# Two-layer macaron block on one core: PSUM banks from a common pool, and the string of steps placed anew

## The chip, the cores and the metric

One core of one Trainium2 chip. The metric is the time of one execution of the program on the device, in microseconds; three runs of the kernel before gave 803.5 to 805.67 us, with a median of 804.64 us.

## The reference, cut to what matters

The input is x of shape (2, 1024, 128), two sequences of 1024 rows. Six residual steps follow each other (`ln` is the layer norm):

```python
x = x + 0.5 * int8_linear(ln(x))              # layer 0: quantised rows, 128x128 weights
x = x + causal_attention(ln(x), H=16, d=8)    # with rotary positions
x = x + 0.5 * int8_linear(ln(x))
x = x + 0.5 * down(silu(gate(ln(x))) * up(ln(x)))   # layer 1: 128 -> 384 -> 128
x = x + causal_attention(ln(x), H=16, d=64)
x = x + 0.5 * down(silu(gate(ln(x))) * up(ln(x)))
```

The two attentions are most of the work: 2 x 16 heads of 1024 x 1024 scores each, of which the lower triangle counts.

## The kernel before, in words

Rows are put in 8 tiles of 128. A start written out by hand (up to about 37 us) takes sequence 0 through the first linear layer and the projections of layer 0; an end written out by hand does the last products of pair 15 and the last FFN of sequence 1. Between them stands `PLAN`, a list of 985 steps. All engines walk this same list in order, and each does its own part of a step: TensorE fills a slot of PSUM, ScalarE ("A") and VectorE ("V") read it, GpSimd and the DMA queues (SP) do what belongs to it. The order comes from the string `ORDER`: each letter takes the next step of its own stream (`streams`).

Layer 0's attention works on 8 groups of 4 heads, layer 1's on 16 pairs of heads (2 sequences x 8). Scores come in 9 chunks of 1024 columns (in a group, twice 9: two heads each):

- `gkq` (a), `gmax` (m), `gturn` (t), `gexp` (e), `gweigh` (w), `gheads` (g): keys and queries turned; scores filled (L1207) and their maxima taken by VectorE (L1054); the maxima turned and moved by DMA into the queries; scores filled once more and exponentiated by ScalarE (L811); their product with the values (L1156), which gathers in bank 7; the heads turned back (L1389).
- `pq`, `pk`, `pv` (Q, K, V), `max` (M), `turn` (T), `exp` (E), `weigh` (W), `sum` (S), `wo` (O): the same for a pair: projections (L1398, L1403), maxima (L1081), exponentials (L840), product with the values (L1177) in banks 6 and 7, sums of exponentials that GpSimd adds up (L672) and TensorE sums over rows (L1238), the output product (L1435). The reciprocals of the sums go out to DRAM and come back spread over the partitions (`reciprocals`, L456, L462), and GpSimd multiplies (L518).
- `h`: the steps of norms (`ln`), linear layers (`xq`, `imm`), rotary positions (`rope`), FFN (`xt`, `up`, `down`) and so on, which lead from one attention to the next: sequence 1's first layers, then 0's middle, 1's middle, and 0's last FFN.

PSUM has 8 banks of 512 fp32 columns. Before, banks 0 to 5 are a ring of three slots of two banks (`RING`), which all steps with readers take in turn, one-bank ones too; bank 6 is a side slot for `gturn`, `gheads`, `xq` and `scale` as long as layer 1's products don't need it (`ON_SIDE`, up to step 457, the first `weigh`). TensorE waits before each fill until the readers of the slot's user before are done:

```python
before = user_before(n)          # three users back in the ring, one back on the side
if before is not None:
    for e in PLAN[before][3]:
        pe.wait_ge(slot_seen[e], READS[e][before])
```

A reader takes the slot's 1024 columns in one instruction, `up` and `gkq` excepted, whose halves go to different places. `KEEP` names steps ahead of which some matmuls (L1246) are put in whose result isn't used.

## Time and profile before

| | |
|---|---|
| time, median of three runs | 804.64 us |
| profiled execution, span | 798.2 us |
| TensorE matmuls busy | 725.3 us, 91% |
| VectorE busy | 532.1 us, 67% |
| ScalarE busy | 450.9 us, 56% |
| GpSimd busy | 466.8 us, 58% |
| instructions | 21288 |

The span goes from the first to the last instruction of one profiled execution; the runs' times hold some 6 us more around it. The engines' shares are means over stages of different kinds, so the rows below take stretches apart. A matmul's busy time overlaps that of the next one, as they are pipelined.

### The profile page before, as it was taken

Reading aid. Unit: us, or ns where it says so; the run is one execution under the profiler, and the core shown is the slowest. Engines: PE = TensorE matmul, PEld = TensorE weight load, DVE = VectorE, ACT = ScalarE, POOL = GpSimd, SP = SyncE. Lnnn points to the kernel's source line nnn. Section 1 sums busy time; section 2 is a strip of 40 time slices with the busy share of each in tenths; the row PEclk is TensorE's granted clock in tenths of the full one; section 3 lists DMA queues with packets and bytes.
Section 4 is the critical chain, followed back from the end, with each engine's and each line's share of the span. In section 5 each row is a group of like instructions: output and inputs, shape, how many; then the busy total and the mean of one; then the engine's idle time right before and its main releaser. Section 6 shows DMA issues by size and latency. Waiting matters only on the chain.

```text
span 798.2 us, 21288 instructions
## 1 busy us (share of the span) xinstructions
PE 725.3 (91%) x9393; PEld 429.3 (54%) x9406; DVE 532.1 (67%) x704; ACT 450.9 (56%) x495; POOL 466.8 (58%) x367
## 2 busy tenths in 40 slices
PE   3667888888888899998999999999999999999997
PEld 1533454445335444554565565555776655676764
DVE  7699967889778765777675575556536556753037
ACT  2424769986575689555636655665444665546312
POOL 6815567600850300499968777877655986667840
PEclk9855989999899999999999999999999999999999
DMA  8000000000000000000001111001101101111110
GB/s 271 2 1 2 3 2 3 2 3 2 2 2 2 2 3 2 2 2 5 27 4 26 29 30 29 10 22 28 30 2 28 29 3 29 29 29 30 28 29 26
DMA packets 13223, 16.18 MB, mean 20 GB/s; under 512 B 3052, under 2 KB 10572, under 8 KB 13132
## 3 DMA queue, kind: packets, MB, share of 16 engines
q1 hardware_dynamic: 12556, 14.50, 6.3%
q8 instruction: 74, 1.21, 0.6%
q10 hardware_dynamic: 576, 0.33, 0.2%
q14 instruction: 17, 0.14, 0.1%
HBM read 13.26 MB, written 1.17 MB: 18 GB/s over the span
## 4 chain that ended last, share of the span: by engine, by line
PE 70%; DVE 17%; POOL 5%; ACT 5%; issue 3%; DMA 0%; ACTq 0%; POOLq 0%; DVEq 0%
PE ps L1228 19%; PE ps L1177 16%; DVE big L1054 9%; PE ps L1156 6%; PE ps L1398 5%; PE ps L1207 5%; PE ps L1435 3%; ACT Pr L811 3%; PE ps L1403 2%; PE ps L1352 2%; PE ps L1238 2%; POOL acts L672 1%; DVE moments L1004 1%; PE ps L1346 1%; PE ps L1318 1%
## 5 line engine op out<-in xcount | busy, mean ns | idle before, releaser
L1081 DVE TENSOR_REDUCE mxb<-ps 128x8 f32<-128x1024 f32 x144 | 173.3, 1222 | 90.4 <-PE ps L1228 61.3
L672 POOL TENSOR_TENSOR V0s<-V0s,Pr 128x1024 f32<-128x1024 f32 x77 | 182.1, 2365 | 62.7 <-ACT Pr L840 31.0
L1054 DVE TENSOR_REDUCE big<-ps 128x8 f32<-128x1024 f32 x144 | 168.9, 1218 | 27.9 <-PE ps L1207 16.6
L811 ACT ACTIVATE Pr<-ps,exp_scale 128x1024 f32<-128x1024 f32 x144 | 154.8, 1114 | 44.4 <-PE ps L1207 31.5
L840 ACT ACTIVATE Pr<-ps,exp_scale 128x1024 f32<-128x1024 f32 x112 | 119.5, 1114 | 90.3 <-PE ps L1228 72.9
L1228 PE MATMUL ps<-big 64*128 64x128 f16 (+2 forms) x2560 | 168.9, 259 | 0.7 <-DVE mxb L1081 0.4
L1207 PE MATMUL ps<-big 32*128 32x128 f16 (+2 forms) x1280 | 102.4, 279 | 35.7 <-DVE big L1054 22.2
L1228 PEld LDWEIGHTS ps<-big 64*128 64x128 f16 x2560 | 92.8, 94 | 71.6 <-issue 17.0
L1177 PE MATMUL ps<-Pr,V1s 128*64 128x128 f32 (+2 forms) x960 | 111.3, 371 | 0.0
L1207 PEld LDWEIGHTS ps<-big 32*128 32x128 f16 x1280 | 40.4, 95 | 108.5 <-DVE big L1054 53.1
L587 POOL TENSOR_TENSOR stats<-moments 128x8 f32<-128x8 f32 x9 | 1.9, 210 | 163.7 <-DVE moments L1004 163.7
L684 ACT ACTIVATE big<-ps 128x1024 f16<-128x1024 f32 (+3 forms) x63 | 51.9, 826 | 71.0 <-PE ps L1398 28.2
L672 POOL TENSOR_TENSOR acts<-acts,Pr 128x1024 f32<-128x1024 f32 x35 | 82.5, 2357 | 13.2 <-ACT wkqv_s L823 4.0
L1156 PE MATMUL ps<-Pr,V0s 128*18 128x128 f32 (+2 forms) x1280 | 82.1, 382 | 0.2 <-ACT Pr L690 0.2
L1177 PEld LDWEIGHTS ps<-Pr,V1s 128*64 128x64 f32 x960 | 56.0, 136 | 37.1 <-issue 24.7
L1077 DVE TENSOR_TENSOR big<-ps,big 128x1024 f16<-128x1024 f32 x32 | 39.1, 1223 | 34.4 <-ACT big L684 33.6
L1228 PE MATMUL ps<-big,shr_s 64*128 64x256 f16 (+2 forms) x384 | 55.8, 287 | 0.0
L518 POOL TENSOR_TENSOR big<-Pr,rec_b 128x1024 f32<-128x1024 f32 x15 | 35.5, 2363 | 17.6 <-DMA rec_b<-scratch_dram 7.5
L1398 PE MATMUL ps<-XT,wqkv 128*128 128x512 f16 x192 | 45.3, 380 | 0.0
L1156 PEld LDWEIGHTS ps<-Pr,V0s 128*18 128x18 f32 x1280 | 30.4, 100 | 20.2 <-issue 13.2
L840 ACT ACTIVATE V0s<-ps,exp_scale 128x1024 f32<-128x1024 f32 x22 | 24.5, 1114 | 18.2 <-PE ps L1218 17.0
L1398 PEld LDWEIGHTS ps<-XT,wqkv 128*128 128x128 f16 x192 | 17.6, 98 | 22.0 <-ACT Pr L840 1.7
(242 smaller groups left out, 921.7 us busy)
## 6 DMA issues: line engine op xcount, KB each, us to landing
rec_b<-scratch_dram SPq DMA_DIRECT2D x30, 256.0 KB, 3.9
X<-in_x_dram SPq DMA_DIRECT2D x2, 256.0 KB, 3.8
big<-in_pick_rows_dram SPq DMA_DIRECT2D x2, 256.0 KB, 3.0
X<-in_x_dram SPq DMA_DIRECT2D x1, 512.0 KB, 5.4
rec_b<-in_w_q_dram SPq DMA_DIRECT2D x1, 512.0 KB, 5.8
XT<-in_w_k_dram SPq DMA_DIRECT2D x1, 512.0 KB, 6.6
XT<-in_w_v_dram SPq DMA_DIRECT2D x1, 512.0 KB, 7.3
wo_s<-in_w_o_dram SPq DMA_DIRECT2D x1, 512.0 KB, 8.1
```

Source lines behind the costliest of these rows:

```text
L672: g.tensor_tensor(dst, dst, src, ALU.add).then_inc(summed, 1)
L684: a.activation(dst, src, ACT.Copy).then_inc(slot_act, 1)
L811: a.activation(group_buf[e_no % GROUP_BUFS], by_head(slot), ACT.Exp, scale=exp_scale[0][:, 0:1]).then_inc(slot_act, 1)
L840: a.activation(dst, by_head(slot), ACT.Exp, scale=exp_scale[1][:, 0:1]).then_inc(slot_act, 1)
L1054: v.tensor_reduce(maxima_of(mall[:, r, 2 * u:2 * u + 2], i), block_view(by_head(slot), i), AX.X, ALU.max, negate=True).then_inc(slot_dve, 1)
L1077: v.tensor_tensor(low, slot, high, ALU.subtract).then_inc(slot_dve, 1)
L1081: v.tensor_reduce(maxima_of(mxb[:, r], arg), block_view(by_head(slot), arg), AX.X, ALU.max, negate=True).then_inc(slot_dve, 1)
L1156: ins = te.matmul(ps[HR * j:HR * j + 2 * VW, 7, a0 - 512 * half:a1 - 512 * half], values(g // GB, t, GH * (g % GB) + j, half), src, start= ...
L1177: ins = te.matmul(ps[h * D1:(h + 1) * D1, 6 + bank, a0 - 512 * bank:a1 - 512 * bank], V1[p % SETS][:, t, h * D1:(h + 1) * D1], src, start= ...
L1207: ins = te.matmul(slot[:, 512 * h + off:512 * h + off + a1 - a0], still[rows, tile(t)], moving[rows, a0:a1], start=q == 0, stop=cut is Non ...
L1228: ins = te.matmul(slot[:, 512 * h + off:512 * h + off + a1 - a0], still[rows], moving[rows], start=q == 0 and k == 0, stop=not goes_on and ...
L1398: ins = te.matmul(slot[:, cols], w16[:, ww], x16[:, xx, cols], start=part == 0, stop=part == 2)
```

## The change

All banks but 7 are in a pool, a list of banks, dealt in turn while the list of steps is walked, before anything runs; a step takes one bank (`ONE_BANK`) or two from its front, and puts them at its end. From the first `weigh` on bank 6 is left out. Since two banks taken one after the other needn't be neighbours, a slot is now a list of banks; readers of a whole slot read it in one instruction if the banks are neighbours in rising order, else in two (`whole`, `copy_whole`). TensorE waits for the last users of each bank (`wait_for_banks`). `v` is read in two halves always. The string `ORDER` and the list `KEEP` are new; the steps in it are the same ones, 985 in all.

```diff
-RING = 3
-SIDE = "gturn", "gheads", "xq", "scale"
+ACC0, ACC1 = 7, (6, 7)
+ONE_BANK = "gturn", "gheads", "xq", "scale", "turn", "sum", "wo"
 ORDER = (
-    "ammmmmmmmammmmmmmmmmmmmtmmmeehmmmaememhehehwmemhwemwmememmeewmhmehwemhwemewtehmmwememewhmeaeewmhmmhm"
-    "hewmemwememgehhhmhhemtwehmeewemewmemhehmhhehwmewmhmwmeamegemeweemwmhwemewmemmeewemmteewmememwmemwmew"
-    "memgeaemewmemwemwememmeewemewemmwemtemwemwmememwmeegmmhmmhhemhwemwmemhehwemewaeehtemwmemwemmmeheehwe"
-    "hmwemwhemhewmemememwewemewmheagemhhhhwhhewmememmhtemwehemwmememmwemhememmhewegemwemwmemwememeweeewtQ"
-    "eKweeweewMeweegMweeVMeweMewMeewMeweeVMweeMwMwgTKhQhEhMEhMWMEWMEEMWMMEWEMhhKQWVMEWTMhMEWWEMWMEMWEMWME"
-    "WhMEEhhVShhEMQKWTWEEMWMMWWMEMWMEEhEEWhhEWhhVhhEMWMQhhKShMWMEMWTEMWWMEMWWEMEWWWMEEEMWMSWThKQVWMEEEMWW"
-    "MEMWMEEEEEEMWWMMMWSQKVTWWWMEMWMEEMWWMESMEMWMMVKQTWWEEEMWMEMWEEMWWEMWWMEMWMEEEEMWWSTQKVWWMEEEEMWMWMMW"
-    "WMEEEEEMWWMEEMSKQVTWWWWMEEMWWMMWEEEKEMWWMEEMWWMMQSWWTMEEMWMMEWWEMVVOMEEEMWSMEEEMWOKOTQOMEMWWWWMMEhWW"
-    "WMEEMWMMEWMEESQKVThWWMEMWMEEMWWMEMWWMEEEEhVWSMEMWWTQhhWKEWEMEhEMWWMMMWWSMEEEEhhWWWMEEMWMhKQVTWWMEEMW"
-    "MWMEMWMEEEKWWMEMWMEQThVEMSEMMWWWMEEMWWWMEEMWWMEEEMWWWTSEEEEWWWWEEEEEESWWOOOOEEWWWWWWW"
+    "ammmmmmmmammmmmmmmmmamtmmehememmmmwhhheemmemmememwmemwememewemhtmhemwheewwehmheweewmeamemememwhemwme"
+    "mwemmhmwmhmehmeewmemememwtmehwmehhhmhmewmemwehmgeemwemewemmwhmhehmgwemeaewheememewmemhwtmehwmememaem"
+    "wmemwememememwememegwhemewmewmemwemwmtememememwemwemegemwhmmhheeweawmememmewhememewhthemwemwmememwme"
+    "hmmewmemhemhewmwemheehweawmemmeememwememehtmmhwemwhhehhhwhewegmehheweeemwemewmhewemewmememwemwemhwem"
+    "eQtKKQewegeMeweMeMeweMewMeewMeweMeweMwMeVegewTQwMgVEMEhEMWWMEMWEMhEEEMWMEWhhMKKVMWhTMWMSWMhEWhEMQWMW"
+    "EVEWMEMWMEMWTMEMWhMEEWMMQEWWhhEEWEMWMMKEWEMWMWMESEhTVMWMWMMEhWEMQKWEEMEWMWTVWEMEWMEMWSWMhEEWEMMWhhWE"
+    "KhEWVMhWhWEhEEWQMhMEWhWTSEMWEMQEKWMhSWEMEMEMWWMMEWMEEMWMWTEEhWEWWMWMEEEQEEWMKMWSWMWMMEWTWEMVEWWMEMWE"
+    "MVEQMWKEWMWEEMWMEWSMTVEEMWMMWQEMWWMEEVEMWEMWKEWEMSMWMWMEWTEMWQEMWWMEEEKEWSMMWMOWMVTEWMOMWEEOMEOMWMEM"
+    "WWMMQKWSEEMWWTEMWEhEEEMWEMMWEQWWWMMVWMEEKWMWhESEWEWTMWMEMWMEEMWhEWVWEhKEWEEMWMEMWMEQhWSWTMEMWMEMWMVM"
+    "WEMWEhWMVEMEEKhWEQSTEWMMWEWMEMWMMWWMEWMEhWEEWMhWEESEWTEEWhWWWEWEEEEWWOEWEESOWWEWOOWWW"
 )
 KEEP = {
-    ('gmax', 1, (7, 1)): 2,
-    ('gmax', 5, (1, 0)): 1,
...
+    ('gexp', 0, (0, 0)): 3,
+    ('gmax', 3, (8, 0)): 2,
+    ('gexp', 2, (6, 1)): 3,
+    ('gexp', 3, (8, 0)): 2,
+    ('gexp', 4, (8, 1)): 2,
+    ('gmax', 6, (4, 1)): 2,
+    ('gmax', 7, (0, 0)): 2,
+    ('gmax', 7, (4, 0)): 2,
 }
-def user_before(n):
-
-    users, back = (SIDE_USERS, 1) if ON_SIDE[n] else (USERS, RING)
-    k = users.index(n) - back
-    return users[k] if k >= 0 else None
+def deal_banks():
+
+    free = [bank for bank in range(8) if bank != ACC0]
+    user, banks_of, users_before = {}, {}, {}
+    for n, (kind, key, arg, readers) in enumerate(PLAN):
+        if (kind, key, arg) == ("weigh", 0, 0):
+            free = [bank for bank in free if bank not in ACC1]
+            users_before[n] = [user[bank] for bank in ACC1 if bank != ACC0]
+        if not readers:
+            continue
+        count = 1 if kind in ONE_BANK else 2
+        taken, free = free[:count], free[count:] + free[:count]
+        banks_of[n] = sorted(taken)
+        users_before[n] = [user.get(bank, -1 - bank) for bank in taken]
+        user.update((bank, n) for bank in taken)
+    return banks_of, users_before
...
+        def whole(n):
+
+            taken = BANKS_OF[n]
+            if taken[1] == taken[0] + 1:
+                return [(slice(0, 2), ps[:, taken[0]:taken[0] + 2, :])]
+            return [(slice(k, k + 1), ps[:, taken[k]:taken[k] + 1, :]) for k in range(2)]
...
+            def copy_whole(n, dst, func=ACT.Copy, scale=1.0):
+
+                act.wait_ge(slot_filled, SLOT_NO[n] + 1)
+                for part, src in whole(n):
+                    ins = a.activation(dst[:, part], src, func, scale=scale)
+                ins.then_inc(slot_act, 1)
...
                 if kind == "gexp":
...
-                    act.wait_ge(slot_filled, SLOT_NO[n] + 1)
-                    a.activation(group_buf[e_no % GROUP_BUFS], by_head(slot), ACT.Exp,
-                                 scale=exp_scale[0][:, 0:1]).then_inc(slot_act, 1)
+                    copy_whole(n, group_buf[e_no % GROUP_BUFS], ACT.Exp, exp_scale[0][:, 0:1])
...
                 if kind == "gmax":
...
-                    v.tensor_reduce(maxima_of(mall[:, r, 2 * u:2 * u + 2], i), block_view(by_head(slot), i), AX.X,
-                                    ALU.max, negate=True).then_inc(slot_dve, 1)
+                    for part, src in whole(n):
+                        ins = v.tensor_reduce(maxima_of(mall[:, r, 2 * u:2 * u + 2][:, part], i), block_view(src, i), AX.X,
+                                              ALU.max, negate=True)
+                    ins.then_inc(slot_dve, 1)
...
+            def wait_for_banks(n):
+
+                for e in "AV":
+                    seen = [READS[e][before] for before in USERS_BEFORE[n] if before >= 0 and e in PLAN[before][3]]
+                    if seen:
+                        pe.wait_ge(slot_seen[e], max(seen))
+                if any(-1 - bank in USERS_BEFORE[n] for bank in ACC1):
+                    pe.wait_ge(first_v_kept, 1)
```

The other readers of whole slots (`xt`, `acts`, `qk`, `pq`, `pk`, `pv`, `exp`, `max`, `wo0`, `down`) are changed in the same way.

## Rows read from the trace of the kernel before

**Rows 1.** The page: busy us, share and instructions; then tenths in 40 slices of 20 us.

```profile
PE 725.3 (91%) x9393; PEld 429.3 (54%) x9406; DVE 532.1 (67%) x704; ACT 450.9 (56%) x495; POOL 466.8 (58%) x367
...
PEclk9855989999899999999999999999999999999999
```

**Rows 2.** Table of stretches: PE, PEld, DVE, ACT, POOL busy us (count); clock; DMA share; GB/s.

```profile
0.00:67.00 67.00, 37.22 (x315) 22.32 (x321) 54.71 (x96) 19.55 (x41) 32.21 (x64) 0.76 0.26 82
67.00:290.00 223.00, 192.40 (x2833) 101.14 (x2836) 184.07 (x246) 159.89 (x166) 95.62 (x109) 0.93 0.01 2
...
375.00:770.00 395.00, 392.37 (x4979) 245.02 (x4975) 218.10 (x238) 209.36 (x222) 295.02 (x159) 1.00 0.09 24
```

**Rows 3.** Waits of TensorE's matmuls, 67 to 290 us: us in total, times, longest us.

```profile
PE ps L1207 <- DVE big L1054: 13.7, 33, 1.1
PE ps L1207 <- ACT Pr L811: 7.1, 15, 1.0
```

**Rows 4.** Waits of TensorE's weight loads, 67 to 290 us.

```profile
PEld ps L1207 <- DVE big L1054: 36.8, 58, 2.1
PEld ps L1207 <- ACT Pr L811: 24.8, 43, 1.7
```

**Rows 5.** Waits of VectorE, 67 to 290 us.

```profile
DVE big L1054 <- PE ps L1207: 16.6, 23, 3.0
DVE big L1054 <- PE ps L1198: 9.2, 8, 3.0
```

**Rows 6.** Groups by line and shape: busy us, mean ns of one, idle before them.

```profile
L1054 DVE TENSOR_REDUCE big<-ps 128x8 f32<-128x1024 f32 x144 | 168.9, 1218 | 27.9 <-PE ps L1207 16.6 <-PE ps L1198 10.3
L811 ACT ACTIVATE Pr<-ps,exp_scale 128x1024 f32<-128x1024 f32 x144 | 154.8, 1114 | 44.4 <-PE ps L1207 31.5 <-PE ps L1198 12.1
L684 ACT ACTIVATE big<-ps 128x1024 f16<-128x1024 f32 x32 | 32.7, 1023 | 28.2 <-PE ps L1398 28.2
L1043 DVE TENSOR_TENSOR ffn_h<-ffn_g,ps 128x512 f32<-128x512 f32 x18 | 12.4, 687 | 0.6
L790 ACT ACTIVATE ffn_g<-ps 128x512 f32<-128x512 f32 x18 | 10.7, 601 | 7.4 <-PE ps L1346 6.2 <-DVE ffn_h L1043 1.2
```

**Rows 7.** Instructions in order of time: reads back to back: start, us.

```profile
157.45 6.90 DVE L1054 TENSOR_REDUCE big<-ps 128x8 f32<-128x1024 f32 x6 [0.67 <-PE ps L1207]
...
299.15 5.16 ACT L811 ACTIVATE Pr<-ps,exp_scale 128x1024 f32<-128x1024 f32 x5
```

**Rows 8.** Instructions in order of time: values kept, an ln, an imm.

```profile
34.25 2.17 ACT L738 ACTIVATE V0s<-ps,stats 128x128 f32<-128x128 f32 x8
...
66.69 1.64 DVE L1004 BATCH_NORM_STATS2 moments<-X 128x6 f32<-128x128 f32 x8
...
89.56 2.16 DVE L1016 SCALAR_TENSOR_TENSOR ffn_h<-ps,stats,wsc_s 128x128 f32<-128x128 f32 x8
```

**Rows 9.** The chain that ended last, in order of time: start, us, what.

```profile
38.03 9.14 DVE big L1054 x8
...
255.72 5.57 PE ps L1352 x48
...
289.68 1.40 PE ps L1398 x6
...
293.04 0.98 PE ps L1156 x8
```

**Rows 10.** Instructions in order of time: the tail.

```profile
759.19 0.94 DVE L1093 RECIPROCAL wkqv_s<-wkqv_s 16x128 f32<-16x128 f32 x1
...
763.53 2.36 POOL L672 TENSOR_TENSOR V0s<-V0s,Pr 128x1024 f32<-128x1024 f32 x1 [0.17 <-POOL V0s L672]
...
766.72 1.06 PE L1238 MATMUL ps<-V0s,ones_s 128*32 128x512 f32 x8
...
768.38 2.37 POOL L518 TENSOR_TENSOR big<-Pr,rec_b 128x1024 f32<-128x1024 f32 x1 [2.49 <-issue]
...
771.48 3.84 PE L1448 MATMUL ps<-wo_s,big 128*128 128x128 f32 x32
```

More of the change, by code:

```diff
@@ L200 @@
 SLOT_NO = [0] + list(accumulate(int(bool(step[3])) for step in PLAN))
-ON_SIDE = [bool(step[3]) and step[0] in SIDE and n < AT["weigh", 0, 0] for n, step in enumerate(PLAN)]
-SIDE_USERS = [n for n, side in enumerate(ON_SIDE) if side]
-USERS = [n for n, step in enumerate(PLAN) if step[3] and not ON_SIDE[n]]
-RING_NO = {n: k for k, n in enumerate(USERS)}
 READS = {e: list(accumulate(int(e in step[3]) for step in PLAN)) for e in "AV"}
@@ L1031, in _ @@
                     dve.wait_ge(slot_act, READS["A"][n])
-                    v.tensor_tensor(x16[:, 1], slot, x16[:, 0], ALU.subtract).then_inc(slot_dve, 1)
+                    for part, src in whole(n):
+                        high, low = (in_banks(x16[:, w])[:, part] for w in range(2))
+                        ins = v.tensor_tensor(low, src, high, ALU.subtract)
+                    ins.then_inc(slot_dve, 1)
                 if kind == "up":
@@ L1076, in _ @@
                     dve.wait_ge(slot_act, READS["A"][n])
-                    v.tensor_tensor(low, slot, high, ALU.subtract).then_inc(slot_dve, 1)
+                    for part, src in whole(n):
+                        ins = v.tensor_tensor(in_banks(low)[:, part], src, in_banks(high)[:, part], ALU.subtract)
+                    ins.then_inc(slot_dve, 1)
                 if kind == "max":
@@ L1080, in _ @@
                     dve.wait_ge(slot_filled, SLOT_NO[n] + 1)
[L1081 to L1082 removed]
+                    for part, src in whole(n):
+                        ins = v.tensor_reduce(maxima_of(mxb[:, r][:, part], arg), block_view(src, arg), AX.X, ALU.max,
+                                              negate=True)
+                    ins.then_inc(slot_dve, 1)
                     if arg == CH - 1:
@@ L1227, in pair_scores @@
                             rows = slice(h * D1, (h + 1) * D1)
-                            ins = te.matmul(slot[:, 512 * h + off:512 * h + off + a1 - a0], still[rows], moving[rows],
+                            ins = te.matmul(slot[h][:, off:off + a1 - a0], still[rows], moving[rows],
                                             start=q == 0 and k == 0,
@@ L1396, in _ @@
                         for half in range(2):
-                            cols = slice(512 * half, 512 * half + 512)
-                            ins = te.matmul(slot[:, cols], w16[:, ww], x16[:, xx, cols], start=part == 0, stop=part == 2)
+                            ins = te.matmul(slot[half], w16[:, ww], x16[:, xx, half_of(half)], start=part == 0, stop=part == 2)
                 if kind == "pv":
+                    pe.wait_ge(slot_dve, read("V", "xt", (4, key // NP), None))
+                    pe.wait_ge(w_split, 3)
                     x16, w16 = X1[:, key // NP], wqkv1[:, 2, :, tile(key % NP)]
@@ L1427, in _ @@
                 if kind == "sum":
[L1428 removed]
+                    ins = add_up(key, slot[0])
                 if kind == "wo":
```

135 lines of the change are left out of this document (61 added, 74 removed).

## The prediction

> **What bounds the kernel now.** I read the totals and the forty slices first, then a table of stretches, then who waits for whom in each. TensorE is busy 91% of the span [rows 1], but the average hides two regimes. Up to 67 us the program starts and the first maxima are taken. From 67 to 290 us, while layer 0's heads run, TensorE is busy 192 of 223 us, VectorE 184, ScalarE 160, and the granted clock is 0.93; from 375 to 770 us, with layer 1's pairs, TensorE is busy 392 of 395 us and VectorE only 218 [rows 2]. So the second regime is bound by TensorE's own work: only 3 us of it aren't covered by a matmul. Nothing that eases PSUM can give much there.
>
> The first regime is bound by slots being emptied. The matmuls of the scores (L1207) wait 13.7 us for a maximum on VectorE and 7.1 us for an exponential on ScalarE, and their weight loads, which run ahead, 36.8 and 24.8 us [rows 3, 4]. In the other direction VectorE waits 16.6 + 9.2 us for scores [rows 5]. VectorE idles 223 - 184 = 39 us of this stretch [rows 2]; since every maximum must still be taken, 39 us is the most that better placing could bring, and the 26 us spent waiting for scores is the part that slots or order could plausibly touch.
>
> **Does the pool give more depth?** That is the disputed point, and it can be counted from the two strings. A two-bank step takes the two banks that have been out longest, and waits for the last user of both. With seven banks, three two-bank steps hold six; the fourth takes the seventh bank, which has been free for longer, and one bank of the third step before it, and waits for that one. A slot is given back as a whole, at the second half's end, so half a slot of spare room is never usable. Before step 457 (the first weigh, when bank 6 leaves the pool), 331 of 333 two-bank fills of the new string that reuse a bank wait for a step with exactly two two-bank fills in between; in the old string it is 329 of 331. After it, three slots against six banks, the new string has 62 waits with only one fill in between and 271 with two, the old one 52 with one, 6 with none and 277 with two. The one-bank steps (16 gturn and gheads before step 457, turn, sum and wo after) no longer cost a slot, but the side bank is gone for them. I take the pool by itself at 0 us; its ends are -2 us (the six waits without a fill in between, 0.3 to 0.4 us each by the wait of a score for its slot [rows 3]) and +1.2 us (the wait at step 457 for one more read).
>
> **What the pool adds: split reads.** A step whose banks aren't neighbours is read by two instructions of 512 columns. Up to step 457 that befalls 15 gmax, 26 gexp, one xt, one acts, one pk and one pv; v is read in halves always; up and gkq were halves before. After it: 9 max, 9 exp, one pv. VectorE: a whole read is 1218 ns alone, a half 687 [rows 6], so a split costs 2 x 687 - 1218 = 156 ns at most; back to back the whole read takes 6.90 / 6 = 1150 ns, and if a half also gains 70 ns of overlap, 2 x 617 - 1150 = 84 ns [rows 7]. ScalarE: whole 1114, a half with an immediate scale 601; the pointer scale adds 1114 - 1023 = 91 ns (Exp against Copy) [rows 6], so 2 x 692 - 1114 = 270 ns at most, and with 82 ns of overlap (5.16 us for five) 2 x 610 - 1032 = 188 ns [rows 7]. The lower ends are nearer, since both halves are queued together: 16 x 0.1 = 1.6 us on VectorE, 31 x 0.19 = 5.9 us on ScalarE before step 457. VectorE's lie on the path wholly (it is the busiest reader); of ScalarE's I take 43 / (43 + 58), the share of ScalarE among the slot waits of the weight loads [rows 4], so 2.5 us. Together +4 us, from +1.5 (half of it hidden by idle time) to +9 (upper prices, all on the path). After step 457 they are covered by TensorE's work, and cost 19 x 0.2 = 3.8 us if that cover were gone.
>
> The row shows that halving a read costs 0.08 to 0.27 us. The Trainium skill says the same kind of thing against this change (VectorE: DVE Perf Modes, "The TRN2 errata"): every instruction pays a fixed latency, 120 cycles at 0.96 GHz for VectorE and 172 at 1.2 GHz for ScalarE out of PSUM, and one should keep tiles at 512 elements or more. By that page the splits would be an estimated 16 x 0.125 + 31 x 0.143 x 0.43 = 3.9 us; by the rows they are 4 us.
>
> **The order.** The kernel has no scheduler at run time: every engine walks the string, so a string with evenly mixed work is worth time. I priced each step by its read: 1.15 us for gmax, 1.03 for gexp [rows 7], 1.22 (VectorE) and 1.02 (ScalarE) for other whole reads, 0.69 and 0.60 for half ones [rows 6], 1.64 for the eight statistics of an ln and 2.16 for an imm's eight [rows 8], on TensorE 0.98 for a gweigh and 5.57 for a down [rows 9], added them per engine over blocks of fifty steps, and let the dearest engine count (VectorE or ScalarE, but for TensorE in the new 330 to 372). Step 29 starts with the ln at 66.8 us and the old string's pq 0 (step 399) at 289.7 [rows 8, 9]: 223 us for a sum of
>
> - old, blocks from 29, 80, 130, 180, 230, 280, 330, 373: 29.1, 24.3, 23.3, 23.5, 27.5, 23.1, 30.3, 13.8 = 194.9 us
> - new, to its own pq 0 at step 401: 26.8, 23.6, 23.2, 23.5, 25.1, 26.3, 26.7, 12.6 = 187.8 us
>
> The old string crowds VectorE where the FFN steps stand (18 gmax and two ln in 230 to 279; 15 gmax, six up, one down and two ln in 330 to 372), and the new one thins the gmax there (9 in 330 to 372). With only three slots of cover, blocks should be shorter: at eight steps (mean over where the blocks begin) the old sum is 213.8 us and the new one, without splits, 207.5. The measured 223 lies above both, so the method sees most but not all of the time. Taken at eight steps: -6.3 us. Bounds: 0 (what is even in the sum may not be even in time) and -12 (half of the 26 us of waits for scores).
>
> From pq 0 to the end of the string both hold the same TensorE work, since all 985 steps are the same ones; the kept-warm matmuls (L1246) go from 19 to 18. Where TensorE is the bound, order is worth nothing: 0, from -3 to +3. The chain of a head step is no tighter: xt (4, 0) moves from step 373 to 396, five steps ahead of pq 0 rather than 26. Its copy and subtraction are 1.02 + 1.22 us [rows 6], against five steps of some 0.6 us; at worst TensorE stands there for 1 us, once. xt (4, 1) has 11 steps ahead of pq 8 where it had 95; there a full 2.2 us is covered by 11 steps.
>
> Moved queues: SP's turn, sum and reciprocal DMAs go along with their steps. **The tail**: the seven additions of pair 15 on GpSimd take 2.36 us each, end at 765.9 us, and may begin only behind weigh (15, 1); the last sums start at 766.7 [rows 10]. Behind weigh (15, 1) the new string has two more exp and a sum, 2.7 us more work, so that wait gets looser. From sum 14 on it has 15.6 us of TensorE work to the last sums and 4.8 us more to the output product (766.7 to 771.5); the reciprocal's way through DRAM takes 759.2 to 770.8 = 11.6 us, plus some 5 us before it: 16.6 against 20.4. Nothing late; 0.
>
> **The start**: the pool hands bank 6 to the fourth fill, the third gmax, which so waits for the first values (L738), copied by 36.4 us, while the first maximum starts at 38.0 [rows 8, 9]: 0.
>
> **Sum.** The profiled execution has a span of 798.2 us, 6.4 below the runs' median of 804.64; I keep that distance. 798.2 + 0 (pool) + 4 (splits) - 6.3 (order) + 0 = 795.9, so 802.3 us in the metric; I forecast 802.
>
> **Rivals.**
> *The order gives more.* A mixed string keeps VectorE fed and lets TensorE arrive at the pairs earlier. For: VectorE's 26 us of waits [rows 5] are long ones, up to 3.0 us, at places where the old string bunches exponentials. Against: 187.8 of work plus splits can't come closer to measured time than the old one did. -12 + 4 = -8: 797, down to 792.
> *Splits cost, order doesn't pay: slower.* In 67 to 290 us nearly each fill waits for the third before it, so a read that is longer by 0.16 or 0.27 us lengthens the cycle of its slot at once. Upper prices: 16 x 0.156 + 31 x 0.27 = 10.9 us, of which some 7 on the path; the order then gives 2. 804.6 + 5 = 809.5. It decides from the point where the order's gain is under 4 us.
> *The change doesn't do what it says.* By the count above the pool frees nothing; if the new string is no better than the old and ScalarE's splits are hidden, 804 to 806.
>
> The granted clock could join any of them: parts of 200 to 250 us ran below full [rows 1], at a loss that is in the 223 us already; the strings give no ground to expect more or less of it, so it has no term.
>
> **Chances.** The forecast (799.5 to 804.5) 0.40, the order giving more 0.22, slower by splits 0.24, nothing at all 0.14. A measurement here tells 0.3%, 2.4 us, from no change; half of the forecast's case is below 802.2. Faster 0.20 + 0.22 + 0.02 = 0.44; within 0.3% 0.18 + 0.10 = 0.28 with the rest of the case of nothing; slower 0.28. The range to hold 8 in 10 goes from 792 to 811.
>
> **What would show it.** Right: VectorE's busy time up by about 2 us, ScalarE's by 6 to 9, with forms of 512 columns at the lines of the maxima and exponentials, 24 and 35 steps' worth; the first pq product near 287 to 289 us; TensorE's stretch from there to the end unchanged within 3 us; slot waits of L1207 not much rarer. Wrong: slot waits that vanish (then the pool has depth after all), a first pq behind 291 us, or TensorE idle within the pairs.

## The result, and the profile after

The changed kernel takes 821.16 us, the median of four runs (817.01 to 822.36), against 805.13 us for the kernel before beside it (803.5 to 805.67): a ratio of 1.0192, with an interval from 1.0164 to 1.0221. It is slower by some 16 us (15.5 by the ratio), where 802 us was forecast.

The page's totals, and the granted clock in 40 slices of 20.5 us, which answer [rows 1]:

```profile
span 818.8 us, 21596 instructions
...
PE 743.1 (91%) x9395; PEld 423.5 (52%) x9405; DVE 536.3 (66%) x729; ACT 459.3 (56%) x536; POOL 466.2 (57%) x367
...
PEclk9955999987998999999999999999999999999999
```

The span grew by 20.6 us. TensorE has as many matmuls as before (9395 against 9393), yet it is busy for 17.8 us longer. VectorE has 25 instructions more and 4.2 us more, ScalarE 41 more and 8.4 us more: these are the split reads.

The table of stretches of the changed kernel, with the columns of [rows 2]:

```profile
67.00:290.00 223.00, 188.02 (x2726) 97.47 (x2731) 179.30 (x239) 158.46 (x188) 95.14 (x109) 0.90 0.01 2
375.00:770.00 395.00, 394.10 (x4848) 227.77 (x4844) 224.57 (x260) 211.49 (x228) 291.37 (x160) 1.00 0.09 22
```

In layer 0 (67 to 290 us) less was done in the same time: 2726 matmuls against 2833, VectorE 179.30 us against 184.07. In layer 1 TensorE is even a little busier than before, 394.10 of 395 us against 392.37, but it got through 4848 matmuls against 4979, 2.6% fewer. By its busy time nothing has changed there; by its count it has. The same holds for the weight loads, 4844 against 4975.

Two marks divide the traces: the first matmul of a `pq` product, and the matmuls that spread the last reciprocals, 28.6 us ahead of the end in nearly all kernels. Instructions in order of time, TensorE, around the first `pq` and around the last reciprocals of the changed kernel:

```profile
298.55 1.47 PE L1433 MATMUL ps<-XT,wqkv 128*128 128x512 f16 x6
...
790.13 1.97 PE L1497 MATMUL ps<-id_s,last_rec 128*64 128x128 f32 x32 [0.80 <-DVE last_rec L1138]
```

And of the kernel before:

```profile
289.62 1.47 PE L1398 MATMUL ps<-XT,wqkv 128*128 128x512 f16 x6
...
769.58 1.97 PE L1460 MATMUL ps<-id_s,last_rec 128*64 128x128 f32 x32 [0.42 <-DVE last_rec L1105]
```

So before, the first `pq` comes at 289.6 us and the pairs take 769.6 - 289.6 = 480.0 us; after, 298.5 and 491.6 us; the rest is 28.6 us in both. Of the 20.6 us of span, 8.9 are lost before the first `pq` and 11.6 behind it, in the stretch in which TensorE is never idle. The second part is the surprise, and the larger one in what follows.

The first `pq` doesn't stand at the same point of the work in every kernel. It is step 399 before and 401 after, and the changed kernel has two `gexp` and two `gweigh` more ahead of it, and one `gheads` and one `gturn` fewer. A part of the 8.9 us is work that has moved, then. The first `weigh` is step 457 in both. TensorE, before and then after:

```profile
328.42 1.09 PE L1177 MATMUL ps<-V0s,V1s 128*64 128x128 f32 x16
```

```profile
337.00 1.95 PE L1218 MATMUL ps<-V0s,V1s 128*64 128x128 f32 x20
```

By this mark 8.6 us are lost ahead of it, and 12.0 between it and the last reciprocals (441.2 us before, 453.1 after). It too favours the new string a little, which has a `pq`, a `max` and an `exp` more ahead of it, and a `wo0` and two `ln` fewer.

What TensorE waited for in layer 0, 67 to 297 us, matmuls first, then VectorE (us in total, times, longest), answering [rows 3, 5] (to 297 us, since the stage ends later):

```profile
PE ps L1248 <- ACT Pr L705: 11.7, 26, 1.0
PE ps L1248 <- DVE big L1082: 10.0, 22, 1.8
```

```profile
DVE big L1082 <- PE ps L1248: 26.0, 37, 2.0
DVE big L1082 <- PE ps L1239: 4.9, 6, 1.7
```

The slot waits are as large as before (21.7 us against 20.8), and have moved from maxima to exponentials: 10.0 against 13.7 us for VectorE, 11.7 against 7.1 for ScalarE. VectorE's own waits for scores are 30.9 us against 25.8. The new order has not thinned them.

### The profile page after: what moved, and what is told of

Read it like the earlier page. It is cut to its first block, busy times and chain, and to the rows that moved or that the text cites. A ratio compares the mean times of both kernels' runs of the same rounds, so it can differ in the third digit from the quotient of the medians.

```text
span 818.8 us, 21596 instructions
## 1 busy us (share of the span) xinstructions
PE 743.1 (91%) x9395; PEld 423.5 (52%) x9405; DVE 536.3 (66%) x729; ACT 459.3 (56%) x536; POOL 466.2 (57%) x367
## 4 chain that ended last, share of the span: by engine, by line
PE 77%; DVE 11%; ACT 7%; issue 2%; POOL 2%; DMA 1%; SPq 0%; ACTq 0%; DVEq 0%; POOLq 0%
PE ps L1269 20%; PE ps L1218 17%; PE ps L1189 8%; DVE big L1082 7%; PE ps L1248 6%; PE ps L1433 5%; ACT Pr L705 4%; PE ps L1472 3%; PE ps L1440 3%; PE ps L1390 2%; PE ps L1279 2%; PE ps L1384 2%; PE ps L1356 1%; PE ps L1259 1%; PE ps L1239 1%
## 5 line engine op out<-in xcount | busy, mean ns | idle before, releaser
L705 ACT ACTIVATE Pr<-ps,exp_scale 128x1024 f32<-128x1024 f32 (+1 forms) x291 | 282.3, 1011 | 157.0 <-PE ps L1269 80.6
L1113 DVE TENSOR_REDUCE mxb<-ps 128x8 f32<-128x1024 f32 (+1 forms) x153 | 174.0, 1156 | 75.7 <-PE ps L1269 58.2
L1082 DVE TENSOR_REDUCE big<-ps 128x8 f32<-128x1024 f32 (+1 forms) x159 | 170.9, 1119 | 33.2 <-PE ps L1248 26.0
L1269 PE MATMUL ps<-big 64*128 64x128 f16 (+2 forms) x2560 | 173.4, 260 | 0.9 <-ACT Pr L705 0.6
L1269 PEld LDWEIGHTS ps<-big 64*128 64x128 f16 x2560 | 89.7, 94 | 89.7 <-issue 37.6
L1218 PE MATMUL ps<-Pr,V1s 128*64 128x128 f32 (+2 forms) x960 | 118.2, 375 | 0.0
L1248 PEld LDWEIGHTS ps<-big 32*128 32x128 f16 x1280 | 43.8, 98 | 107.8 <-ACT Pr L705 41.8
L1218 PEld LDWEIGHTS ps<-Pr,V1s 128*64 128x64 f32 x960 | 53.4, 136 | 35.5 <-issue 22.6
L1107 DVE TENSOR_TENSOR big<-ps,big 128x1024 f16<-128x1024 f32 (+1 forms) x33 | 39.2, 1192 | 45.4 <-ACT big L705 45.1
L1269 PE MATMUL ps<-big,shr_s 64*128 64x256 f16 (+2 forms) x384 | 55.8, 287 | 0.0
L705 ACT ACTIVATE big<-ps 128x1024 f16<-128x1024 f32 (+1 forms) x33 | 32.8, 997 | 26.5 <-PE ps L1433 26.4
L533 POOL TENSOR_TENSOR big<-Pr,rec_b 128x1024 f32<-128x1024 f32 x15 | 35.5, 2366 | 12.5 <-DMA rec_b<-scratch_dram 8.9
L1189 PEld LDWEIGHTS ps<-Pr,V0s 128*18 128x18 f32 x1280 | 31.3, 103 | 20.6 <-issue 12.9
L699 ACT ACTIVATE big<-ps 128x512 f32<-128x512 f32 (+2 forms) x31 | 19.4, 624 | 30.1 <-PE ps L1402 15.8
L705 ACT ACTIVATE V1s<-ps,v_back 128x1024 f32<-128x1024 f32 (+1 forms) x18 | 18.1, 1018 | 25.0 <-PE ps L1440 25.0
```

Source lines behind the costliest of these rows:

```text
L533: g.tensor_tensor(YT[:, p % NP], y_raw[p % 2], rec_b[:], ALU.mult).then_inc(normed, 1)
L705: ins = a.activation(dst[:, part], src, func, scale=scale)
L1082: ins = v.tensor_reduce(maxima_of(mall[:, r, 2 * u:2 * u + 2][:, part], i), block_view(src, i), AX.X, ALU.max, negate=True)
L1107: ins = v.tensor_tensor(in_banks(low)[:, part], src, in_banks(high)[:, part], ALU.subtract)
L1113: ins = v.tensor_reduce(maxima_of(mxb[:, r][:, part], arg), block_view(src, arg), AX.X, ALU.max, negate=True)
L1189: ins = te.matmul(ps[HR * j:HR * j + 2 * VW, ACC0, a0 - 512 * half:a1 - 512 * half], values(g // GB, t, GH * (g % GB) + j, half), src, sta ...
```

## The experiments

Each ratio is against the kernel before on the same chip; the experiments ran on three chips, so losses in us are worked out from the ratios and not from the medians. The last three columns come from each kernel's trace.

| kernel | ratio, interval | median us | first `pq` | from it to the last reciprocals | from the first `weigh` to them |
|---|---|---|---|---|---|
| before, in the profile shown | | 804.64 | 289.6 | 480.0 | 441.2 |
| after | 1.0192 [1.0164, 1.0221] | 821.16 | 298.5 | 491.6 | 453.1 |
| e1_order | 1.0155 [1.0114, 1.0196] | 816.53 | 294.0 | 492.5 | 454.2 |
| e2_pool | 1.0023 [1.0000, 1.0046] | 806.58 | 294.8 | 481.6 | 441.0 |
| e3_late | 1.0199 [1.0153, 1.0245] | 820.69 | 296.0 | 492.6 | 454.2 |
| e4_early | 1.0056 [1.0028, 1.0084] | 809.83 | 297.2 | 482.2 | 441.7 |
| e5_before_b | one run | 805.65 | 295.2 | 480.1 | 441.3 |
| e6_grouped_b | 1.0727 [1.0658, 1.0796] | 860.09 | 292.1 | 532.1 | 490.0 |
| e7_grouped_old_b | 1.0520 [1.0471, 1.0569] | 846.76 | 291.1 | 521.0 | 474.5 |
| e8_scattered_b | 1.0442 [1.0399, 1.0484] | 839.88 | 294.0 | 514.2 | 474.7 |
| e9_full | 1.0318 [1.0295, 1.0342] | 830.48 | 293.8 | 505.3 | 466.4 |
| e10_half | 1.0034 [1.0016, 1.0051] | 808.23 | 294.2 | 482.6 | 443.8 |
| e11_gentle | 1.0307 [1.0256, 1.0358] | 828.49 | 295.1 | 503.6 | 465.1 |
| e12_gentle_old | 1.0075 [1.0046, 1.0104] | 810.56 | 292.0 | 485.4 | 443.9 |
| e13_late_back | 1.0089 [1.0060, 1.0118] | 811.72 | 293.7 | 481.8 | 441.1 |
| e14_warm | 1.0046 [1.0025, 1.0067] | 807.62 | 300.1 | 480.3 | 441.2 |

One thing must be read from this table before any cause is. The kernel before (twice, with e5), e3, e7, e8, e9, e10 and e12 run the same ring and the same string up to step 398, the last `gturn`, and this step still falls anywhere from 289.4 us (before) to 295.0 (e5), 292.6 in the mean of these eight traces. In e3 the first `pq`, at 296.0 us, is step 403, four steps behind this `gturn`, so it isn't the same point of the work as 289.6 before. The `gturn` in e3:

```profile
292.19 0.24 PE L1376 MATMUL ps<-idh_s,big 128*64 128x128 f16 x1
```

The trace on which the prediction rested was a quick one, by some 3 us. So one trace says little about the early stage below 3 us or so. The late stage is steady: with the old order there it is 480.0 to 482.2 us from the first `pq`, and 441.0 to 441.7 from the first `weigh`, in six traces (the kernel before twice, e2, e4, e13, e14).

### The two parts of the change, apart

The order without the pool: the kernel before, with the new `ORDER` and `KEEP`.

```diff
 ORDER = (
-    "ammmmmmmmammmmmmmmmmmmmtmmmeehmmmaememhehehwmemhwemwmememmeewmhmehwemhwemewtehmmwememewhmeaeewmhmmhm"
+    "ammmmmmmmammmmmmmmmamtmmehememmmwhhheemmemmememwemwememewemhtmhemwheewwehmheweewmeamemememwhemwme"
...
```

> The kernel before, with its ring, side bank and whole reads, but with the new string and its list of kept-warm matmuls. Theory O (the string is the cause: in the pairs it changes 401 times between matmuls of different tile shape instead of 262, at 0.097 us for each in both traces, and layer 0 loses some 7 us with more time at the low clock): 13 to 17 us slower than before. Theory P (the pool is the cause: split reads, waits for two users): within 3 us of before.

Measured: 1.0155, +12.5 us, with 492.5 us in the late stage. With the ring still in place, all of the late loss is there.

The pool without the order: the changed kernel, with the old strings.

```diff
 ORDER = (
-    "ammmmmmmmammmmmmmmmamtmmehememmmwhhheemmemmememwemwememewemhtmhemwheewwehmheweewmeamemememwhemwme"
+    "ammmmmmmmammmmmmmmmmmmmtmmmeehmmmaememhehehwmemhwemwmememmeewmhmehwemhwemewtehmmwememewhmeaeewmhmmhm"
...
```

> The changed kernel with its pool and split reads, but with the old string and its kept-warm matmuls; this string splits more maxima (23 gmax, 21 gexp before the first weigh, 7 max, 9 exp, 8 projections after). Theory O: 1 to 5 us slower than before, the price of the splits in layer 0. Theory P: 12 to 17 us slower.

Measured: 1.0023, +1.9 us, from 0 to 3.7. The pool gives no depth and costs a little, as its split reads do. Both parts together, 12.5 + 1.9 = 14.4 us, come near the 15.5 of the change.

### The order, in two halves

Late half new: the kernel before, its own string up to step 398, from there the remaining steps as the new string has them.

```diff
-    "eKweeweewMeweegMweeVMeweMewMeewMeweeVMweeMwMwgTKhQhEhMEhMWMEWMEEMWMMEWEMhhKQWVMEWTMhMEWWEMWMEMWEMWME"
+    "weeQKKQeweeMeweMeMeweMewMeewMeweMeweMwMeVegewTQwMgVEMEhEMWWMEMWEMhEEEMWMEWhhMKKVMWhTMWMSWMhEWhEMQWMW"
```

> The kernel before, ring and kept-warm matmuls too, with its own string up to step 398 and the new string's order for all that is left: 400 changes of tile shape behind step 400 instead of 262. Theory O with the price of a change: 138 x 0.097 = 13 us slower, all of it behind 290 us, TensorE busy there all along. If the late order costs nothing and all is lost early: within 2 us of before.

Measured: 1.0199, +16 us, 492.6 us in the late stage. Early half new: the kernel before with the new string up to step 400 (and the new `KEEP`), the old order for the rest.

```diff
-    "ammmmmmmmammmmmmmmmmmmmtmmmeehmmmaememhehehwmemhwemwmememmeewmhmehwemhwemewtehmmwememewhmeaeewmhmmhm"
+    "ammmmmmmmammmmmmmmmamtmmehememmmwhhheemmemmememwmemwememewemhtmhemwheewwehmheweewmeamemememwhemwme"
```

> The kernel before with the new string up to step 400 and its kept-warm matmuls, and the old string's order for the rest (259 changes of shape there). Theory O: 4 to 8 us slower than before, with the first pq product some 6 us later than 289.7 us and more time at the lower clock between 85 and 290 us; behind it as before. If only changes of shape matter (180 against 182 up to step 400): within 1 us of before.

Measured: 1.0056, +4.5 us, 482.2 us in the late stage. So the late order costs 12 to 13 us by the traces where the prediction had put 0 +- 3, and the early one doesn't gain the 6.3 that it was to gain. The two halves add up to 16.0 + 4.5 = 20.5 us where the whole order cost 12.5. The late stages agree (454.2 us from the first `weigh` in e3 and in e1), so the 8 us lie ahead of it. Two parts of them can be named. Where the two strings are joined in e4, a `gheads` and a `gturn` follow each other (steps 401 and 402), and TensorE waits 1.52 us between them, which it doesn't in e1:

```profile
296.99 0.24 PE L1371 MATMUL ps<-idh_s,big 128*64 128x128 f16 x1 [1.52 <-DVE acts L1063]
```

And e4's ten executions had a mean granted clock of 0.947, the 19 of the kernel before beside them 0.953. Over the 53 executions of the kernel before beside the experiments, the time goes with that mean, from 807.7 us at 0.945 to 800.0 at 0.958; a straight line through them gives 0.42 us for 0.001, an estimate of 2.5 us for e4, from a correlation alone. The 4 us that remain are no more than the three intervals allow (3.3 us either way for e1, 3.7 for e3, 2.3 for e4).

What differs late? TensorE does not idle in either kernel. From 375 to 765 us, the table of stretches of before and then of after (columns as in [rows 2]):

```profile
375.00:765.00 390.00, 388.51 (x4931) 242.48 (x4927) 217.84 (x237) 207.85 (x220) 292.51 (x158) 1.00 0.08 23
```

```profile
375.00:765.00 390.00, 389.10 (x4798) 224.46 (x4793) 224.14 (x259) 210.38 (x227) 286.71 (x158) 1.00 0.09 23
```

The clock is 1.00 in both. The waits of the weight loads are put down to "issue", nothing that the profile shows, and there are more of them for the scores. 375 to 765 us, before, then after:

```profile
PEld ps L1177 <- issue: 27.2, 94, 0.8
PEld ps L1228 <- issue: 13.9, 42, 0.8
```

```profile
PEld ps L1269 <- issue: 30.5, 71, 0.8
PEld ps L1218 <- issue: 24.9, 80, 0.8
PEld ps L1433 <- issue: 5.8, 14, 0.8
```

The chain of waits of the changed kernel, 500 to 512 us, shows what a product with the values costs among scores (L1218 is `weigh`, L1269 scores; start, us, matmuls):

```profile
499.98 0.45 PE ps L1269 x16
500.42 0.23 PE ps L1259 x6
500.65 1.88 PE ps L1218 x20
502.53 0.32 PE ps L1269 x4
502.86 1.02 PE ps L1218 x16
503.88 2.92 PE ps L1269 x34
```

A `weigh` alone between scores takes 1.02 us; two in a row take 1.88, not 2.04. (Each of them covers the same 1024 columns; the number of matmuls goes by the widths of its pieces, and is 16 for one and 4 for the other.) The second one is cheaper by 0.16 us, and two changes of the kind of matmul have fallen away with it. I measured the gap from the end of the last columns to the next matmul's start over all such changes in both traces: its median is 0.092 us from scores to `weigh`, 0.098 back, and 0.095 to 0.099 from and to the projections. Within scores it is about nothing. Added up from the first `pq` to the last reciprocals, the gaps at changes of shape are 31.3 us before (279 changes in the trace) and 43.2 after (410): 11.9 us more, in a stretch that is 11.6 longer. A gap is about as long as one weight load of the scores, 94 ns on average; that of `weigh` takes 136, and the gap ahead of a `weigh` is no longer for it (weight loads by shape, 375 to 765 us, kernel before):

```profile
L1228 PEld LDWEIGHTS ps<-big 64*128 64x128 f16 x2224 | 80.9, 94 | 59.1 <-issue 13.9 <-ACT Pr L840 10.6 <-DVE mxb L1081 5.7
L1177 PEld LDWEIGHTS ps<-Pr,V1s 128*64 128x64 f32 x858 | 50.3, 136 | 33.8 <-issue 23.1 <-ACT Pr L840 2.7 <-ACT ffn_g L790 0.4
```

The theory, then: as long as matmuls keep one tile shape (64 rows of the array for scores, all 128 for the projections, 128 rows by 64 columns for `weigh`) the next load hides behind the running matmul, and each change of shape has a price of its own, perhaps one load in the open. Behind step 400 the old string changes shape 262 times and the new one 401 times; up to step 400 it is 182 and 180. 139 x 0.096 = 13.3 us would be the whole late loss. The rival: these gaps are waits for slots that the trace puts down wrongly, so that it is the order of the reads that matters.

### Fewer and more changes of shape

The theory was first tested by order alone. e5 is the kernel before once more, for a second trace of it.

> The kernel before, unchanged, for a second trace of it. If the trace of before was of a quick execution (its first pq product at 289.6 us, while the late-order kernel, whose program is the same up to there, had it at 296.0): a first pq product some us later than 289.6, and the same 480 us from there to the spreading of the last reciprocals within 1 us. If that stage is steady: 289.6 within 1 us.

Measured: 805.65 us, the first `pq` at 295.2 us and 480.1 us from it to the last reciprocals. The late stage is steady, the early one is not.

e6 is the changed kernel, and e7 the kernel before, with `max`, `exp` and `weigh` steps behind step 402 moved by up to three places so that like stands by like: 263 changes instead of 401, and 188 instead of 262. e8 is the kernel before with the same steps moved by up to four places so that they mix: 401 instead of 262. One line of e7's string:

```diff
-    "MWMEMWMEEEKWWMEMWMEQThVEMSEMMWWWMEEMWWWMEEMWWMEEEMWWWTSEEEEWWWWEEEEEESWWOOOOEEWWWWWWW"
+    "EMWWWEMEEMMKWWWMEMEQThVSEEMWWWMMEMMEWWWMEMEWWEEEMMWWWTSEEEEWWWWEEEEEESWWOOOOEEWWWWWWW"
```

> The changed kernel, pool and all, with the max, exp and weigh steps behind step 402 moved by at most 3 places so that steps of one tile shape stand together: 263 changes of shape behind step 400 instead of 401. Price of a change 0.097 us: 13 us faster than the changed kernel (some 808 us), the stretch from the first pq product to the last spreading 478 to 481 us instead of 491.6. If changes of shape only come along with something else (order of the head steps, slots of two users): within 3 us of the changed kernel.

> The kernel before with its ring, and the max, exp and weigh steps behind step 402 moved by at most 3 places: 188 changes of shape instead of 262. Price of a change 0.097 us: 7 us faster than before, the stretch from the first pq product to the last spreading 473 us instead of 480. If grouped maxima and exponentials then wait for slots: a gain of under 3 us, with waits of the pairs' scores on ScalarE and VectorE that before has not.

> The kernel before with its ring, and the max, exp and weigh steps behind step 402 moved by at most 4 places the other way, so that shapes alternate: 401 changes instead of 262. Price of a change 0.097 us: 13.5 us slower than before, all of it between the first pq product and the last spreading. If the new late order is slow for where it puts the head steps and not for the changes: within 3 us of before.

Measured: 1.0727, 1.0520 and 1.0442. The first two are slower by far where they should have been faster, and the third loses 34 us where 13.5 were expected. Their tables show why; e7, 375 to 765 us, its matmuls' waits there, and the chain of waits from 514 us:

```profile
375.00:765.00 390.00, 362.43 (x4506) 217.97 (x4503) 218.88 (x247) 196.36 (x207) 264.99 (x148) 1.00 0.08 21
```

```profile
PE ps L1228 <- ACT Pr L840: 8.1, 18, 0.9
PE ps L1228 <- DVE mxb L1081: 6.7, 15, 0.9
```

```profile
514.46 1.67 PE ps L1228 x56
516.13 0.23 PE ps L1218 x6
516.35 0.25 PE ps L1228 x4
516.61 1.10 ACT Pr L840
517.71 0.05 issue
517.75 0.84 PE ps L1228 x24
```

TensorE is idle for 27.6 us of this stretch, where before it was 1.5. Fills of scores in a row ask for a slot that hasn't been given back, and TensorE stands for 1.1 us until the exponential is read. A `weigh` takes no slot of the ring: set between scores, it is what TensorE does while a slot is emptied. Moving it aside saves changes and takes away that cover. Summed over the runs of successive score fills in the late stage, TensorE's idle time within them, counted from the last column of one matmul to the start of the next, is 2.4 us before, 3.3 after, 34.3 in e6, 41.4 in e7 and 9.8 in e8. For e7 the bill reads 41 - 2 of new waits less 74 x 0.096 = 7: +32 of the 41 us. For e8 it is 13.3 + 7.4 = 21 of its 34 us, and for e6, against the changed kernel, 31 - 13 = 18 of 40.5. The rest is the same kind of wait where it falls on a change of shape: what those gaps hold beyond 0.1 us each is 5.8 us before and 4.2 after, but 20.7 in e6, 10.6 in e7 and 17.6 in e8. With it, and with the gaps between other matmuls of one shape (4.6 us more in e7, 6.1 in e6, 1.0 in e8), the three sums come within 1 us. So these runs don't measure the price of a change by themselves; they show the other side of the trade.

### The price of a change, by itself

To change the count and nothing else, a matmul whose result isn't used goes ahead of each `exp` fill that follows a `max` or `exp`, behind step 402, 119 times, into the slot that the fill then overwrites. The order stays that of the kernel before. With all 128 rows of the array (e9) it makes two changes of shape each time; with 64 rows, as the scores have (e10), none. Both stream 64 columns. The difference of the two kernels is one number:

```diff
+CLOSE = [(n, step[0]) for n, step in enumerate(PLAN) if step[3] or step[0] in ("weigh", "gweigh")]
+PROBED = {n for (_, before), (n, kind) in zip(CLOSE, CLOSE[1:])
+          if n >= 402 and kind == "exp" and before in ("max", "exp")}
...
+                if n in PROBED:
+                    rows = slice(0, P)        # e10: slice(0, D1), 64 rows
+                    te.matmul(slot[:, 0:64], shr[rows], cutq0[rows, 0, 0:64], start=True, stop=True)
```

> The kernel before with 119 small matmuls put in behind step 402, each ahead of an exp that follows a max or exp: 128 rows by 64 columns, their result unused and overwritten. Each puts a matmul of another tile shape between two of 64 rows, so 238 changes of shape more. Theory L (a change of shape costs a weight load, 94 to 98 ns, that isn't hidden under the matmuls before it): 119 x 27 ns for the columns + 238 x 0.095 = 3 + 23 = 26 us slower than before. If an own shape costs nothing: 3 us slower.

> The same 119 matmuls at the same places, but of 64 rows, the shape of the scores on either side. Theory L: their weight loads are hidden like those of the scores, 3 us slower than before, the 27 ns of columns each; at most 119 x 0.12 = 14 us if loads on the same 64 rows are exposed. The difference to the kernel with 128 rows is what a change of shape costs.

Measured: +25.6 us and +2.7 us. The same 119 matmuls cost nearly ten times as much when their shape differs: (25.6 - 2.7) / 238 = 0.096 us for a change, and by the traces' late stages (505.3 - 482.6) / 238 = 0.095. The table of stretches, e9 and then e10:

```profile
375.00:765.00 390.00, 388.39 (x4758) 227.53 (x4758) 220.61 (x238) 205.39 (x213) 273.53 (x152) 1.00 0.08 21
```

```profile
375.00:765.00 390.00, 387.86 (x4979) 252.01 (x4978) 221.39 (x243) 207.56 (x221) 290.59 (x159) 1.00 0.08 23
```

Busy time and clock are the same within 0.6 us, and e9 does 221 matmuls fewer: the same signature as that of the changed kernel. The chain of waits shows the single case (L1306 is the added matmul, L1230 the scores); e9, then e10:

```profile
507.11 0.32 PE ps L1230 x4
507.43 0.14 PE ps L1306
507.57 1.19 PE ps L1230 x10
```

```profile
501.36 0.32 PE ps L1230 x4
501.68 0.03 PE ps L1306
501.71 1.08 PE ps L1230 x10
```

0.14 against 0.03 us for the added matmul, and 1.19 against 1.08 for the ten scores behind it: 0.11 each time, one in, one out. The rival of misread slot waits is out, since neither the slots nor the order differ here. What the 0.096 us are spent on is not shown: an exposed weight load would fit the 94 ns of a load of 128 columns, but no row shows the load by itself at a change.

The Trainium skill (TensorE: Matmul & The Clock Gate, "The mechanism") says that "LDWEIGHTS overlaps with in-flight MATMULs only when row_grp differs". By that sentence, a load into all 128 rows behind a matmul in 64 of them meets that matmul's rows and would stand in the open, and 0.096 us against the 94 ns of a load fits; but the second of two `weigh` in a row, with the same rows, costs 0.86 us (1.88 - 1.02) and the first 1.02, so a load between equal shapes is hidden in this trace, which that sentence alone wouldn't give.

### Can the changes be had cheaper?

Gentler moves: e11 is the changed kernel with 65 `weigh` steps moved by one or two places (318 changes instead of 401), e12 the kernel before with 19 moved so (236 instead of 262).

```diff
-    "EVEWMEMWMEMWTMEMWhMEEWMMQEWWhhEEWEMWMMKEWEMWMWMESEhTVMWMWMMEhWEMQKWEEMEWMWTVWEMEWMEMWSWMhEEWEMMWhhWE"
+    "EVEWMEMWMEMWTMEMWhMEEMMWQEWWhhEEEMWWMMKWEEMMWWMESEhTVMMWWMMEhEMWWQKEEMEMWWWTVEMEWMEMWWSWMhWEEEMMhhWWE"
```

> The changed kernel with 65 weigh steps behind step 402 moved by one or two places, and nothing else: 318 changes of shape instead of 401. Theory L without a loss of cover: 83 x 0.097 = 8 us faster than the changed kernel, 1.009 times before. If a weigh that stands between two scores also covers the wait for a slot (theory C, from the kernels grouped by three places, which stood inside their scores for 34 to 41 us instead of 2 to 3): less gain than that, down to a loss of 10 us, with the gaps inside the scores longer than the changed kernel's 3.3 us.

> The kernel before with 19 weigh steps behind step 402 moved by one or two places: 236 changes of shape instead of 262. Theory L: 2.5 us faster than before. Theory C: within 1 us of before, or slower by some us, for the old string already stands where either costs the same.

Measured: 1.0307 and 1.0075, both slower than what they were made from (1.0192 and 1). e11's late stage is 12.0 us longer than that of the changed kernel, though 83 changes, 8 us, were saved; the idle time within its score groups is 21.5 us against 3.3. In e12 it is 11.7 against 2.4, for 26 changes saved. The table of e11 and its waits:

```profile
375.00:765.00 390.00, 376.20 (x4644) 220.15 (x4642) 219.46 (x256) 202.26 (x221) 281.47 (x156) 1.00 0.08 22
```

```profile
PE ps L1269 <- ACT Pr L705: 4.7, 12, 0.9
```

Even moves of one place uncover slot waits. The old string is at 262 changes and 2.4 us of such waits at once; neither of my ways of moving steps kept both.

### The change with its late part taken back

The changed kernel, pool and early order kept, with the old order from step 400 on (259 changes):

```diff
-    "eQtKKQewegeMeweMeMeweMewMeewMeweMeweMwMeVegewTQwMgVEMEhEMWWMEMWEMhEEEMWMEWhhMKKVMWhTMWMSWMhEWhEMQWMW"
+    "egtQKeeewMeweegMweeVMeweMewMeewMeweeVMweeMwMwgTKhQhEhMEhMWMEWMEEMWMMEWEMhhKQWVMEWTMhMEWWEMWMEMWEMWME"
```

> The changed kernel, pool, split reads and its kept-warm matmuls, with the new string up to step 400 and the old string's order for the rest (259 changes of shape there instead of 401). If the late order is what costs and acts alike in pool and ring: the stretch from the first pq product to the last spreading 481 to 484 us instead of 491.6, so 9 to 12 us faster than the changed kernel, 1.005 to 1.009 times before. If pool and new late order need each other: less than 4 us faster.

Measured: 1.0089, and 481.8 us in the late stage. 15.5 - 7.2 = 8.3 us of the loss come back with the late order, 9.8 in the trace's stretch; from the first `weigh` on it takes 441.1 us, as the kernel before does. What is left, 7.2 us, are the splits (1.9 by e2), the early order, and the joint of the strings, at which TensorE waits 0.88 us here.

For the early order one cause could be tried, the clock: its granted mean from 85 to 290 us is 0.95 in the profile of before, but 0.92 in e5, the same kernel, and 0.93 after, in e4, e9 and e14. e14 is e4 with one unused matmul more ahead of each of 22 `gmax` (steps 160 to 199 and 236 to 261):

```diff
+    ('gmax', 3, (7, 1)): 1,
-    ('gmax', 3, (8, 0)): 2,
+    ('gmax', 3, (8, 0)): 3,
+    ('gmax', 3, (8, 1)): 1,
```

> The kernel before with the new string up to step 400 (4.5 us slower than before in the run of that kind) and one more unused matmul ahead of each of the 22 gmax of steps 160 to 199 and 236 to 261, where its trace showed the clock at 1.2 GHz. If the early loss is the clock: those stretches at 2.4 GHz, the first pq product at 293 to 295 us instead of 297.2, at most 1.003 times before. If it is how maxima and exponentials are placed: no faster, the first pq at 297 or later, whatever the clock does.

Measured: 1.0046 against e4's 1.0056. Its trace has the same clock of 0.93 from 85 to 290 us and the first `pq` at 300.1 us, but it is of one of its slowest executions. Over its ten executions the mean clock is 0.953, as in the kernel before, against e4's 0.947; the 22 matmuls of 512 columns add up to an estimated 22 x 0.216 = 4.8 us of TensorE's own time (matmuls of 512 columns start 0.216 us apart in the late stage of before), so a gain by the clock could be eaten up by them. The run neither confirms nor refutes the clock as the cause.

None of these kernels beats the kernel before; the pool with the old order, within 0.5% of it, comes nearest.

## Why the prediction was wrong, and where it was right

**The failed step is "Where TensorE is the bound, order is worth nothing: 0, from -3 to +3."** It took the late stage's 395 us as work that is the same whatever its order, because the matmuls are the same ones and TensorE is busy 392 of 395 us. The work of a matmul is the same, but what is paid between two isn't: 0.096 us at each change of tile shape (e9, e10), and the new string has 139 more of them. That gives 13.3 us; the traces' late stages say 11.6 (after), 12.5 (e1) and 12.6 (e3), or 12.0, 13.0 and 13.0 from the first `weigh`; taking it back gave 9.8 (e13), 12.0 from the first `weigh`. The signal was in the trace of before: weight loads at L1177 and L1228 wait 27.2 and 13.9 us for "issue", and each change from scores to `weigh` and back shows the gap. I read "busy" as "working", and didn't compare what a visit costs alone and in a row. The matmuls' modelled ends overlap the next start, so the gap counts as busy.

The Trainium skill (Perfetto Trace Analysis, "Identifying the Most-Contended Engine") calls matmul busy time a bad measure and wants MFU and the weight loads' busy share instead. Here that share does show that something is lost, though not how much: 242.48 of 390 us before, 224.46 after (7% less, where the count of matmuls is 2.7% less), with busy time at 388.5 and 389.1.

**The order in layer 0, -6.3 us: wrong in size; whether it costs anything is open.** With only the early part new the kernel is 4.5 us slower (e4), of which 1.5 are the wait at the joint of the strings and an estimated 2.5 go with a lower clock, and e13 leaves 5.3 us beyond the splits; e1, whose 12.5 us are all in its late stage, leaves nothing, and e1 less e3 would leave a gain. The sums of reads per block, 187.8 against 194.9, did not turn into time: VectorE's waits for scores are 30.9 us against 25.8, and waits for exponentials rose from 7.1 to 11.7 [rows 3, 5]. A balance of sums over blocks doesn't see who stands before whom within three slots. What the new order does there is open; e14 didn't settle it, and a stage whose end scatters by 5.6 us between traces of one program makes it hard to.

**No depth from the pool, 0 us: right.** 21.7 us of slot waits stand against 20.8, and e2 is 0.2% slower rather than faster.

**Splits, +4 us from 1.5 to 9: the right mechanism, half the size.** e2 has +1.9 us, with the old string, which splits about as many reads. Their prices were right: the halves take 684 ns on VectorE and 688 on ScalarE with the pointer scale (I had 687 and 692), and the pairs, queued together, 1.26 us against a whole read's 1.11. Reads by shape, 60 to 770 us, and one pair in order of time:

```profile
L705 ACT ACTIVATE Pr<-ps,exp_scale 128x512 f32<-128x512 f32 x66 | 41.8, 688 | 10.7 <-PE ps L1248 6.4 <-PE ps L1269 3.1 <-PE ps L1239 1.1
```

```profile
158.12 1.26 ACT L705 ACTIVATE Pr<-ps,exp_scale 128x512 f32<-128x512 f32 x2 [0.17 <-PE ps L1248]
```

ScalarE's busy time rose by 8.4 us, as forecast (6 to 9), VectorE's by 4.2 rather than 2. What was too high is the part that lies on the path, or the clock hid some of it: e2's ten executions had a mean clock of 0.956 against 0.953. The upper end was added up wrongly: the upper prices come to 16 x 0.156 + 31 x 0.27 = 10.9 us, as the rival has it, not to 9.

**Splits behind step 457 covered, tail 0, start 0: right.** e2's late stage is 481.6 us against 480.0 and 480.1; from the last reciprocals to the end it is 28.6 us before and after.

**The rival "splits cost, order doesn't pay", 809.5 us,** had the right sign, but put all of the loss into layer 0, and ended 12 us short, by the amount of the late stage. Of the signs that were to show the prediction wrong, one came, the first `pq` behind 291 us (298.5); but e5 shows that it would have come without any change, at 295.2. The sign to rely on, the late stage unchanged within 3 us, failed: it is 11.6 us longer.

The distance from span to metric, 6.4 us, was a second, smaller flaw: an execution's own time is 1.75 to 1.88 us above its span in every run of which both are known. The other 4.6 us of the 6.4 aren't time around the span, as the section on the profile before has it, but the trace's execution being quicker than its kernel's median.

## What to carry to other kernels

When TensorE is busy throughout, count the changes of tile shape in its stream, multiply by the price of one (0.096 us here), and compare a step's time alone among others with its time in a row of its like. But don't group for that alone: the odd step out may be what TensorE does while a PSUM slot is emptied, and with three slots its removal brought waits of 2 to 5 times what the saved changes gave (18 against 8 us in e11, 39 against 7 in e7). Take a second trace of the kernel before, before you build a sum on one stage of the first.
